# Spread of pi and scores as products on 32 rows, one set of four banks, and new orders in the attention stage

## The reference, cut to what matters

```python
# attention, 12 heads of 64; n is the token within an item
w      = (layernorm(h) @ w_qkv)                        # 64 x 93 x 768
logits = sum(w_normed * w_normed, -1) * temp           # w_normed: w over its norm along n
Pi     = softmax(logits, -1)                           # along n, one per head and token
Pi_n   = Pi / (Pi.sum(-1) + 1e-8)
dots   = einsum('bhn,bhnd->bhd', Pi_n, w * w)
h      = h + (-(w * Pi) / (1 + dots)) @ w_out + b_out
# sparse feed-forward: 8 groups, 64 experts each, the best 4 are used
z      = einsum('nd,sdr->nsr', layernorm(h), P)        # 8 x 16
scores = einsum('nsr,smr->nsm', z, C)                  # 8 x 64
topv, topi = top_k(scores, 4);  gates = softmax(topv)
# then, in a last stage: the chosen experts, summed by gates, two small products, residual
```

## Time and profile before

| | |
|---|---|
| two runs | 1407.14 and 1412.56 us, median 1409.85 |
| profiled execution | 1408.9 us; its span from first to last instruction 1406.8 us |
| busy over the span | PE 1237.8, DVE 1101.4, ACT 1093.7, POOL 1015.5 us |
| mean granted TensorE clock | 0.949 |

### The profile page before, as it was taken

How to read it: one execution, slowest core, us unless ns; L and a number is a source line. 1 busy time by engine, 2 the same in 40 slices (tenths; PEclk the granted TensorE clock), 3 DMA queues, 4 the chain that set the end, 5 groups by cost and what they waited for, 6 DMA issues and landing times.

```text
span 1406.8 us, 34237 instructions
## 1 busy us (share of the span) xinstructions
PE 1237.8 (88%) x12232; PEld 622.3 (44%) x12232; DVE 1101.4 (78%) x3359; ACT 1093.7 (78%) x2708; POOL 1015.5 (72%) x735
## 2 busy tenths in 40 slices
PE   4742799999999999858999999999999999999996
PEld 3741466666666666533333333333333333333332
DVE  5574378888888888866888888888878888888883
ACT  0232557677767776538999999999999999999994
POOL 6661356775677567626888988888798888879894
PEclk8965799999999999968999999999999999999997
DMA  9644312322232222133224232222413322231410
GB/s 273 141 113 85 63 33 73 99 65 68 74 98 65 68 74 89 55 84 102 55 52 94 56 78 63 56 68 55 100 38 81 75 59 64 56 87 44 91 38 12
DMA packets 95704, 107.05 MB, mean 76 GB/s; under 512 B 12772, under 2 KB 92668, under 8 KB 95254
## 3 DMA queue, kind: packets, MB, share of 16 engines
q1 hardware_dynamic: 91184, 96.00, 26.5%
q10 hardware_dynamic: 2240, 5.08, 2.2%
q0 software_dynamic: 2112, 3.79, 1.1%
HBM read 67.88 MB, written 33.71 MB: 72 GB/s over the span
## 4 chain that ended last, share of the span: by engine, by line
ACT 29%; PE 11%; POOL 7%; DVE 4%; issue 4%; POOLq 0%; DVEq 0%; ACTq 0%
ACT ring L1068 19%; ACT arena L1080 9%; POOL arena L821 5%; PE code L1741 5%; PE ring L1728 4%; DVE arena L1476 4%; PE ring L1760 2%; POOL arena L829 1%; POOL arena L827 1%; ACT arena L1076 0%; ACT arena L1088 0%; PE ring L1751 0%; POOLq L157 0%; PE ring L1578 0%; PE ring L1626 0%
## 5 line engine op out<-in xcount | busy, mean ns | idle before, releaser
L1476 DVE TENSOR_TENSOR arena<-ring,arena 128x496 f32<-128x496 f32 x1008 | 611.6, 668 | 132.6 <-ACT ring L1068 131.8
L821 POOL TENSOR_TENSOR arena<-arena 128x992 f32<-128x992 f32 x264 | 608.4, 2316 | 113.5 <-ACT arena L1080 103.5
L1068 ACT ACTIVATE ring<-ring 128x496 f32<-128x496 f32 x1008 | 543.8, 689 | 11.8 <-PE ring L1728 10.8
L1728 PE MATMUL ring<-arena,w_stack 99*32 99x496 bf16 x6144 | 428.2, 375 | 25.6 <-DVE arena L1476 19.7
L1741 PE MATMUL code<-arena,w_pad 128*32 128x496 f32 x3072 | 389.0, 580 | 3.6 <-ACT arena L1084 3.3
L1728 PEld LDWEIGHTS ring<-arena,w_stack 99*32 99x32 bf16 x6144 | 159.8, 95 | 414.6 <-DVE arena L1476 252.4
L1080 ACT ACTIVATE arena<-ring 128x992 f32<-128x992 f32 x252 | 282.6, 1121 | 3.5 <-POOL arena L821 2.9
L1570 PE MATMUL ring<-arena 96*128 96x372 f32 x384 | 135.3, 490 | 1.6 <-ACT arena L924 0.9
L1741 PEld LDWEIGHTS code<-arena,w_pad 128*32 128x32 f32 x3072 | 96.6, 110 | 53.4 <-DVE arena L1476 17.8
L757 POOL TENSOR_TENSOR arena<-arena 128x372 f32<-128x372 f32 x96 | 91.9, 986 | 33.2 <-DVE arena L1316 33.2
L1570 PEld LDWEIGHTS ring<-arena 96*128 96x128 f32 x384 | 71.8, 194 | 62.4 <-ACT arena L932 15.8
(11 more groups left out here) (140 smaller groups left out, 1467.1 us busy)
## 6 DMA issues: line engine op xcount, KB each, us to landing
arena<-gates SPq DMA_DIRECT2D x48, 496.0 KB, 6.7
gates<-arena SPq DMA_DIRECT2D x16, 744.0 KB, 11.5
arena<-h_scratch SPq DMA_DIRECT2D x32, 279.0 KB
arena<-z_parts SPq DMA_DIRECT2D x144, 62.0 KB, 2.7
h_scratch<-arena SPq DMA_DIRECT2D x16, 279.0 KB
z_parts<-arena SPq DMA_DIRECT2D x48, 93.0 KB, 2.1
arena<-h_scratch SPq DMA_DIRECT2D x12, 372.0 KB
out_h<-arena SPq DMA_DIRECT2D x12, 372.0 KB
```

Of the source, the lines that this page charges most:

```text
L821: p_.tensor_tensor(spaces[quad % SPACES][:, j:j + 2], hid[:, POOL_DUOS.index(duo) % 2], gst[:, block // EB, j:j + 2], ALU.mult).then_inc(s ...
L1068: a_.activation(product, product, ACT.Gelu_apprx_tanh).then_inc(s_hid, 1)
L1476: v_.tensor_tensor(spaces[quad % SPACES][:, j + p], duo_bank(duo, p), gst[:, block // EB, j + p], ALU.mult).then_inc(s_gat, 1)
L1728: mm = t_.matmul(bank[32 * q:32 * q + 32], w1s[:, x + 32 * q:x + 32 * q + 32], zst[:, o, j + p], start=True, stop=True)
```

## The change

What it does:

- `spread_pi`: instead of one product of 128 rows by 376 columns per chunk, four products on 32 rows each (item b's rows of `headsel` and of pi), 94 columns, into four banks `ring[:, b]`. The first five chunks lie side by side in each bank, the sixth goes over the first once DVE has read all five. The tiles `pis`, `unitsel` and the steps `pi_placed`, `pi_scale_placed` are gone.
- `scores`: per subtile four products on 32 rows (two groups of z each) by 128 columns, into the same four banks; `scores_copy` reads across them, after all three subtiles are done.
- `w_product` uses the four banks in turn. So W, spread and scores share banks 0 to 3; logits, bias codes, gate scales, the third gates' transpose and a third of the out product share one (`banks[2]`), z and the rest of the out product another (`code_bank`).
- `mean_term` moves from DVE to POOL, as two steps (`nm`, then times `rs`).
- All five `pass_` functions are written anew; the passes go one or two further. The biggest moves: scores, their copies and two of three top-8 now come between the W copies and the softmax; x0 is read one pass earlier by DVE; bias and scales of a unit come a pass later.
- The table load for Gelu is asked for after the last small exponential.

```diff
 def gt_bank(s):
-    return (banks[0], banks[1], pair1[:, 1])[s]
+    return banks[s]
 ...
 # sp.pass_sp
-    if has(u3): store_codes(u3); store_bias(u3); store_scales(u3)
     if has(n2): load_x0(n2)
+    if has(u4): store_scales(u4)
+    if has(u3): store_gates(u3)
+    if has(u2): store_codes(u2)
     if has(u1): store_h1(u1)
     if has(n1): load_xr(n1)
-    if has(u2): store_gates(u2)
+    if has(u3): store_bias(u3)
 ...
 # pool.rstd, and the step moved from dve
+    p_.tensor_scalar_mul(nm[k], mv[k][:, :, 0], -1.0).then_inc(s_nmean[k], 1)
     p_.tensor_scalar_add(ve[k], mv[k][:, :, 1], eps).then_inc(s_ve[k], 1)
 ...
+def mean_term(k, u):
+    pool.wait_ge(s_nmean[k], u + 1)
+    pool.wait_ge(s_rs[k], u + 1)
+    p_.tensor_tensor(nb[k], nm[k], rs[k], ALU.mult).then_inc(s_nb[k], 1)
 ...
 # pool.pass_pool, after:
+    attended(u1, 2..5); z_rest(u2); shift(u2, 0); shift(u2, 1); z_part3(u2); rstd("A", n2)
+    residual_biased(u0); rstd("G", u1); mean_term("G", u1); w2_pi(u0, 0); mean_term("A", n2)
+    w2_pi(u0, 1..5); shift(u2, 2); attended(u0, 0); attended(u0, 1)
 ...
 # act
 def scores_copy(u, s):
-    act.wait_ge(s_sp, SUB * u + s + 1)
+    act.wait_ge(s_sp, SUB * (u + 1))
 ...
-    a_.copy(sc[:, s, :, 0:M], banks[2][0:ST, :].rearrange("p (a b) -> p a b", a=S)).then_inc(s_sc, 1)
+    a_.copy(sc[:, s, :, 0:M].rearrange("p (j a) b -> p j a b", j=PAIRS),
+            ring[0:ST, 0:PAIRS, 128 * s:128 * s + 128].rearrange("p j (a b) -> p j a b", a=2)).then_inc(s_sc, 1)
 ...
 # act.pass_act, after:
+    w_copy(u1, 3..5); z_copy(u3); z_part1(u3); top4_exp(u4); scores_copy(u3, 0); scores_copy(u3, 1)
+    z_part2(u3); scores_exp(u3, 0); scores_copy(u3, 2); logits_exp(u1); gates_copy(u4, 2)
+    scores_exp(u3, 1); gates_copy(u3, 0); gates_copy(u3, 1); copy_bias(u4); norm("G", u2)
+    copy_xT("A", u0); norm("A", n1); w_copy(u0, 0); copy_scales(u4); w_copy(u0, 1)
+    copy_xT("G", u2); scores_exp(u3, 2); w_copy(u0, 2)
 ...
 # dve
 def w_pi(u, c):
-    dve.wait_ge(s_pb, CH * u + c + 1)
-    pb = pair0[:, c % 2, 0:UB * (N + 1)].rearrange("p (b n) -> p b n", b=UB)
+    dve.wait_ge(s_pb, CH * u + (5 if c < 5 else 6))
+    x = (N + 1) * (c % 5)
+    pb = ring[:, 0:UB, x:x + N + 1]
 ...
 # dve.pass_dve, after:
+    dots_scaled(u1); bn_stats_x0(n2); dots_negated(u1); top4(u3, 2); neg_attn(u1); mark(u3, 2)
+    norms_floored(u0); norms_inverted(u0); top4_shifted(u3); head_weights(u0); raw(u3, 2)
+    top4_summed(u3); bn_aggr("A", n2); scales_made(u3); top8(u2, 0); logits_tempered(u0); top8(u2, 1)
+    top4(u2, 0); logits_max(u0); mark(u2, 0); pi_recip(u0); top4(u2, 1); pi_made(u0); raw(u2, 0)
+    pi_sum(u0); mark(u2, 1); pi_sum_eps(u0); residual(u1, 0); pi_complete(u0); raw(u2, 1)
+    residual(u1, 1); bn_stats_h1(u1); bn_aggr("G", u1); w_pi(u0, 0..4); attn_dots(u0, 0); w_pi(u0, 5)
+    attn_dots(u0, 1..3); top8(u2, 2); attn_dots(u0, 4); attn_dots(u0, 5)
 ...
 # pe
 def w_product(u, c):
-    if c < 2: wait(pe, s_rsc, CH * (u - 1) + 5 + c)
-    else:     wait(pe, s_wsq, CH * u + c - 1)
-    o = pair0[:, c % 2, 0:UT]
+    if c == 0: wait(pe, s_rsc, CH * u)
+    if c >= 4: wait(pe, s_wsq, CH * u + c - 3)
+    o = ring[:, c % 4, 0:UT]
 ...
 def scores(u, s):
     if s == 0:
         pe.wait_ge(s_zf, u + 1)
-        pe.wait_ge(s_h1, 2 * (u + 1))
-    wait(pe, s_sc, SUB * u + s)
-    t_.matmul(banks[2][0:ST, :], zf[:, ST * s:ST * s + ST], cbd, start=True, stop=True).then_inc(s_sp, 1)
+        wait(pe, s_wsq, min(CH * (u + 3), CH * UNITS))
+        wait(pe, s_rsc, min(CH * (u + 2), CH * UNITS))
+    for j in range(PAIRS):
+        rows = slice(32 * j, 32 * j + 32)
+        last = t_.matmul(ring[0:ST, j, 128 * s:128 * s + 128], zf[rows, ST * s:ST * s + ST],
+                         cbd[rows, 128 * j:128 * j + 128], start=True, stop=True)
+    last.then_inc(s_sp, 1)
 ...
 def spread_pi(u, c):
     pe.wait_ge(s_pix, u + 1)
-    ...
-    t_.matmul(pair0[:, c % 2, 0:UB * (N + 1)], headsel[:, c], pis.rearrange("p b n -> p (b n)"),
-              start=True, stop=True).then_inc(s_pb, 1)
+    if c == 0:
+        pe.wait_ge(s_wsq, CH * (u + 1))
+        wait(pe, s_sc, SUB * (u - 1))
+    if c == 5: pe.wait_ge(s_rsc, CH * u + 5)
+    x = (N + 1) * (c % 5)
+    for b in range(UB):
+        rows = slice(32 * b, 32 * b + 32)
+        last = t_.matmul(ring[:, b, x:x + N + 1], headsel[rows, c], pix[rows], start=True, stop=True)
+    last.then_inc(s_pb, 1)
 ...
 # pe.pass_pe, after:
+    out_product(u2, 2); gates_transposed(u3, 0); spread_pi(u1, 0..4); bias(u4); gates_transposed(u3, 1)
+    scales_transposed(u4); transposes("A", u0); spread_pi(u1, 5); w_product(u0, 0); w_product(u0, 1)
+    transposes("G", u2); w_product(u0, 2..5); z_product(u2); scores(u2, 0..2); logits(u0)
+    out_product(u1, 0); gates_transposed(u3, 2); out_product(u1, 1)
```

More of the change, by code:

```diff
@@ L973, in logits_exp @@
                 a_.activation(pe_, lg, ACT.Exp, bias=nmax, accum_out=psm).then_inc(s_pe, 1)
-            def pi_placed(u):
-                act.wait_ge(s_pi, u + 1)
-                wait(act, s_pb, CH * u)
-                for b in range(UB):
-                    rows = slice(32 * b, 32 * b + 32)
-                    last = a_.copy(pis[rows, b, 0:N], pi[rows])
-                last.then_inc(s_pip, 1)
             def scores_exp(u, s):
@@ L1043, in pass_act @@
-                if has(u0):
-                    pi_placed(u0)
-                if has(u2):
-                    gates_copy(u2, 2)
-                if has(n1):
-                    copy_xT("A", n1)
-                if has(u1):
-                    norm("G", u1, h1)
-                    copy_xT("G", u1)
-                    z_copy(u1)
-            for i in range(-1, UNITS + 2):
+            for i in range(-1, UNITS + 4):
                 pass_act(i)
-            a_.activation(psm[0:1], psm[0:1], ACT.Gelu_apprx_tanh)
@@ L1453, in pass_dve @@
                     top8(u2, 0)
+                if has(u0):
+                    logits_tempered(u0)
+                if has(u2):
+                    top8(u2, 1)
                     top4(u2, 0)
+                if has(u0):
+                    logits_max(u0)
+                if has(u2):
                     mark(u2, 0)
-                    top8(u2, 1)
+                if has(u0):
+                    pi_recip(u0)
+                if has(u2):
                     top4(u2, 1)
-                    mark(u2, 1)
-                    raw(u2, 0)
-            for i in range(-1, UNITS + 3):
+                if has(u0):
+                    pi_made(u0)
+                if has(u2):
+                    raw(u2, 0)
+                if has(u0):
+                    pi_sum(u0)
+                if has(u2):
+                    mark(u2, 1)
+                if has(u0):
+                    pi_sum_eps(u0)
+                if has(u1):
+                    residual(u1, 0)
+                if has(u0):
+                    pi_complete(u0)
+                if has(u2):
+                    raw(u2, 1)
+                if has(u1):
+                    residual(u1, 1)
+                    bn_stats_h1(u1)
+                    bn_aggr("G", u1)
+                if has(u0):
+                    w_pi(u0, 0)
+                    w_pi(u0, 1)
+                    w_pi(u0, 2)
+                    w_pi(u0, 3)
+                    w_pi(u0, 4)
+                    attn_dots(u0, 0)
+                    w_pi(u0, 5)
+                    attn_dots(u0, 1)
+                    attn_dots(u0, 2)
+                    attn_dots(u0, 3)
+                if has(u2):
+                    top8(u2, 2)
+                if has(u0):
+                    attn_dots(u0, 4)
+                    attn_dots(u0, 5)
+            for i in range(-2, UNITS + 3):
                 pass_dve(i)
@@ L1575, in bias @@
                 pe.wait_ge(s_gc, SUB * (u + 1))
-                wait(pe, s_lt, u + 3 if has(u + 2) else UNITS)
+                pe.wait_ge(s_h1, min(2 * (u + 3), 2 * UNITS))
                 for j in range(PAIRS):
-                    mm = t_.matmul(pair1[32 * j:32 * j + 32, 0, 0:UT], b2p[:, j], gh[:, j], start=True, stop=True)
+                    mm = t_.matmul(banks[2][32 * j:32 * j + 32, 0:UT], b2p[:, j], gh[:, j], start=True, stop=True)
                 mm.then_inc(s_bp, 1)
@@ L1672, in pass_pe @@
                 if has(u2):
-                    scores(u2, 0)
+                    transposes("G", u2)
                 if has(u0):
@@ L1676, in pass_pe @@
                     w_product(u0, 3)
+                    w_product(u0, 4)
+                    w_product(u0, 5)
                 if has(u2):
+                    z_product(u2)
+                    scores(u2, 0)
                     scores(u2, 1)
[L1679 to L1680 removed]
+                    scores(u2, 2)
                 if has(u0):
[L1682 to L1688 removed]
+                    logits(u0)
                 if has(u1):
                     out_product(u1, 0)
[L1692 removed]
+                if has(u3):
+                    gates_transposed(u3, 2)
+                if has(u1):
```

(2 more changed lines are left out.)

309 lines of the change are left out of this document (130 added, 179 removed).

## The result

| | before | after |
|---|---|---|
| median | 1409.85 us | 1460.03 us (1457.13 and 1462.93) |
| profiled execution, its span | 1408.9, 1406.8 us | 1462.93, 1461.2 us |
| busy over the span, PE, DVE, ACT, POOL | 1237.8, 1101.4, 1093.7, 1015.5 us | 1211.1, 1100.0, 1069.9, 1031.2 us |
| mean granted clock | 0.949 | 0.908 |

The ratio is 1.036, with a 95% interval of 1.033 to 1.039: slower by 50 us, where 1403 us was forecast. The stretches of the changed kernel, as in the earlier trace rows (us, busy us of PE, PEld, DVE, ACT, POOL, granted clock, DMA share, GB/s): one unit, from spread to spread, then the start, the thirteen units in the middle, and the end of the stage.

The account below looks back on a forecast made before the run. Bound: a closed chain through several engines, three legs summing to 27.9 us per unit against 28.2. 1408.9 - 3 (13 units) - 6 (start) - 2 (end) + 5 (clock) = 1403 us; range 1365 to 1458.

Parts of the forecast that it names:

- the load of x0: Issued 7.6 us into the unit, data at 13.3; DVE waits 2 us with 3 to spare, so no cost.
- floored norms, inverse and head weights (1.7): DVE steps between W's squares and the softmax, taken as 1.7 us from the earlier trace.
- leg 3: From floored norms to the next spread, nearly all on DVE: 10.9 us forecast against 8.6 before.
- leg 1: From pi complete, where PE starts the spread, to the first W product: 6.4 us forecast against 6.5 before.
- leg 2: From first W product to floored norms, ACT copying and squaring six W chunks: 10.6 us forecast against 13.1.
- the POOL way: POOL's path from pi complete to the first W product, through residual, power, norm and transposed copy: 6.4 us.
- the price of a spread product: PE time of one spread product on 32 rows: 0.2 to 0.3 us, hidden behind DVE up to 0.36.
- the second rival: Slower: loads of the 32-row products follow each other, 0.9 us each, unit 31.7 us, 1458 us; chance 0.12.
- The third rival: Slower: next unit's first gate copy waits for the gates' store; 11.5 us landing gives 1466 us; chance 0.07.
- Start and end: Attention stage outside the 13 steady units: 6 us off at the start, 2 off (0 to 5) at the end.
- The clock: PE's clock may fall between spread and W products, 1.25 us late; a third of 13 units, 5 us added.
- The fourth rival: PE's clock falls in every unit, 13 x 1.25 instead of 5 us: 1414 us; chance 0.06.

Follow-up runs that it names:

- the added products: Changed kernel with x0 loaded early, scale store ahead, one head-weights instruction, plus six unread PE products per unit in the gaps: 1398.98 us, ratio 0.994.
- the last run: Changed kernel with x0's statistics four steps later on DVE, scale store ahead, one head-weights instruction, unread PE products in full passes only: 1397.57 us, ratio 0.992.

## Why the prediction was wrong

**The step that failed** is the load of x0, "costed at nothing". Its working was close: issued 7.1 us into the unit (7.6 was forecast), DVE ready at 10.4 (11.2), data at 14.5 (13.3). DVE waited 4.13 us instead of 2. My limit was 14.2 (0.9 later), so it was passed by 0.3 us. Had that been all, it would have cost little: the floored norms came at 17.3 us, 0.3 after the forecast. What I did not ask is who stands behind DVE's wait. Behind it stood the step that releases `attended`, and `attended` on POOL makes DVE's head weights slow. The same statistics four steps later, with the same late load, gave back 33 of the 50 us.

**The second part of the step** is the term "floored norms, inverse and head weights (1.7)" of leg 3: 3.6 us, which is the 4.1 from 427.55 to 431.65 less 0.5 for the top-4 between them. Leg 3 took 13.8 us instead of 10.9: 2.6 more for the head weights, 0.3 for a shifted top-4 (0.59 instead of 0.26), and 0.9 in which the spread waited for PE, whose out products ran late, less 0.9 by which the other steps, the floored norms among them (0.20 instead of 0.87), were shorter than my sum. A sign was to be seen in the earlier trace rows: a step of 24 columns that takes 0.18 or 0.87 us. I used its two values as bounds and did not ask what the long one waits for. In 14 of its 16 instances it takes 0.86 us or more, and each of these ends 0.03 to 0.04 us after a POOL product that reads SBUF, the `shift` (L752); no run tests it further. For the unit of the earlier trace rows, where the floored norms end at 432.08:

```profile
430.91 1.13 POOL L752 TENSOR_TENSOR arena<-arena 124x512 f32<-124x512 f32 x1 [2.53 <-DVE arena L1248]
```

For the head weights, which have two inputs, the Trainium skill, "SBUF — State Buffer", section "Who interferes with whom", says that a DVE instruction with two inputs in SBUF and a GpSimd instruction that reads SBUF exclude each other for a whole instruction. The traces agree: 0.22 us alone, 0.83 beside `attended` (0.78 per POOL product), 1.00 beside longer POOL products (1.04). At the price that these traces show, it would as a rival have given 13 x 2.6 = 34 us more.

**Leg by leg** (410.29, 416.06, 427.55, 441.35): leg 1 5.8 us (6.4 forecast), leg 2 11.5 (10.6), leg 3 13.8 (10.9). Leg 2's 0.9 is DVE's order, which came to the floored norms only at 427.55, when the mark behind the late statistics was done; the last squares of W were there at 426.56. PE was busy 78% of the unit (80% forecast). DVE was busy without a gap from the floored norms to pi, as forecast: there the loss shows as a longer instruction and not as a wait. Two of the prediction's sums are off: the POOL way's terms of leg 1 add up to 6.5 and not 6.4 us, and if what DVE loses at the floored norms is 0.87 less 0.18, the upper bound of a unit is 29.3 and not 28.5 us. Both stay well under the 31.5 us per unit that were measured on the average of the thirteen.

**Right**: the price of a spread product (0.26 us; 0.2 to 0.3 forecast), so the second rival is out. By the Trainium skill, "TensorE: Matmul & The Clock Gate", section "LDWEIGHTS (loading the stationary operand)", as the prediction used it, eight loads in a line would be 0.85 us (an estimate from its figure of 107 ns for one). In the trace a load of the spread is not short (median 0.19 us), but the forty of five products are over in 1.21 us, so they run beside each other:

```profile
L1617 PEld LDWEIGHTS ring<-arena x768: 181/186/332, 159.8 to 634.6; 32*128 32x128 f32 x192
```

The third rival is out too (landing 3.6 us in the median; 6.2 was its limit), and the two steps moved to POOL took 0.25 and 0.20 (0.25 each). That the measured time is close to what these two rivals gave (1458 and 1466 us) is chance.

**Start and end**: -6 was forecast and +5 came, at least in part for the same cause, since DVE waits up to 9.6 us for x0 in the first units; with the load early the third spread comes between 209.56 and 214.76, against 214.60 before. The end: -2 forecast, +6.6 measured, some 5 of it the scale store behind the loads. I had costed SP's new order for the gates' store only.

**The clock**: once the x0 wait and the store are mended, the time is 1414.14 us. The fourth rival gave 1414, but by a clock that falls in every unit at 1.25 us each; here units of 26.8 us stand beside units of 30.2, so the match is chance. I had held 5 us for the clock; the added products gave 14.

Without these losses (the wait ahead of `attended`, the place of the scale store, the clock), the chain that was forecast is there: 27.3 us per unit against 27.9 forecast and 28.2 before. In the unit of the last run that starts at 409.47 the floored norms come 17.1 us after the spread (17.0 forecast) and the next spread 9.9 us after them (10.9). The 1397.57 us are no test of the 1403, though, since that run also has one head-weights instruction and the added products on PE, which the forecast did not price. What was not run: how much of the 7.4 us of x0's load is due to the load of xr and how much to the bias store.

## What to carry to other kernels

Where a change moves a step that can wait, list what stands behind it on its engine, and then what the engines that it releases will run beside; in these runs each of DVE's small products from SBUF cost about one POOL instruction where POOL's products ran at the same time. A step with two very different durations in a trace is a question to settle before forecasting, not a bound. A stage with shorter PE work can lose its clock and give part of the gain back (14 us here).

## What was not expected of the hardware

- DVE's product of 128 x 72 elements: 0.22 us alone, 0.83 beside POOL's products of 128 x 372, 1.00 beside longer ones; one of 128 x 288 has a median of 1.06 beside them and takes 0.46 alone. The wait is paid once per instruction.
- A load behind a store on the same queue: x0's load (279 KB) takes 5.8 us with nothing just ahead of it, 7.4 behind the load of xr (279 KB) and the bias store (186 KB), 9.5 when it is issued straight behind the bias store.
- PE's granted clock fell in the unit with gaps of 0.50, 0.66, 0.52 and 1.26 us ahead of the W products (0.89 over the unit, first W products 4.46 us instead of 2.77). It stayed at 1.00 in its neighbour with gaps of 0.66 and 1.01 us there, and over twelve units whose gaps ahead of the W products, the scores and the logits were filled with products.
